# A hand-ordered transformer layer on one core: slots reordered so that rounded products stand together

## The reference

```python
q = (hidden_states @ wq).reshape(b, s, H, D)        # also k, v with 4 heads
q = q * cos + _rotate_half(q) * sin                 # also k
q = q / (jnp.linalg.norm(q, axis=-1, keepdims=True) + EPS) * query_scale
scores = jnp.tanh(scores / CAP) * CAP               # window of 128, softmax
out = jnp.einsum('bhqk,bkhd->bqhd', attn, v).reshape(b, s, H * D)
return out @ wo
```

## Time and profile before

| what | value |
|---|---|
| median of three executions | 858.28 us |
| the profiled execution's own time | 859.33 us |
| its span, first to last instruction | 857.6 us |
| mean granted TensorE clock | 0.985 of full speed |
| TensorE busy (matmul) | 809.3 us, 94%, 5118 instructions |
| VectorE (DVE) | 578.5 us, 67% |
| ScalarE (ACT) | 388.3 us, 45% |
| GpSimd (POOL) | 355.3 us, 41% |
| HBM read and written | 18.47 MB and 2.11 MB, 24 GB/s over the span |

### The profile page before, as it was taken

The page is one execution under the profiler, slowest core; times in us unless marked ns, Lnnn a source line. Parts: engine busy times, 40 slices in busy tenths (PEclk is TensorE's granted clock), DMA queues, the critical chain, the costliest instruction groups (busy, mean ns, idle before and its releaser), DMA issues. The chain is left out here.

```text
span 857.6 us, 14062 instructions
## 1 busy us (share of the span) xinstructions
PE 809.3 (94%) x5118; PEld 716.0 (83%) x5118; DVE 578.5 (67%) x1161; ACT 388.3 (45%) x593; POOL 355.3 (41%) x485
## 2 busy tenths in 40 slices
PE   8889999999999999999999999599979999999996
PEld 7678988988888888888888888498868888888885
DVE  3688688488487577578568576857684565555657
ACT  3565655555555455455455554342322333332321
POOL 2787677477577567568468463100000000000000
PEclk8999999999999999999999999799999999999999
DMA  8200000000000000000000000200300101100001
GB/s 323 88 26 8 27 25 1 2 7 2 1 8 1 1 7 2 1 8 1 1 7 2 2 1 1 74 1 20 104 12 26 37 1 38 37 1 1 2 25 74
DMA packets 7587, 21.48 MB, mean 25 GB/s; under 512 B 1496, under 2 KB 3672, under 8 KB 7392
## 3 DMA queue, kind: packets, MB, share of 16 engines
q1 hardware_dynamic: 6944, 20.31, 7.0%
q10 hardware_dynamic: 576, 0.28, 0.1%
HBM read 18.47 MB, written 2.11 MB: 24 GB/s over the span
## 5 line engine op out<-in xcount | busy, mean ns | idle before, releaser
L574 PE MATMUL ps_o<-vaug,probs 128*128 128x129 f32 x1024 | 136.8, 277 | 16.7 <-DVE o_rows L1050 14.4
L574 PEld LDWEIGHTS ps_o<-vaug,probs 128*128 128x128 f32 x1024 | 128.9, 192 | 26.0 <-issue 18.9
L825 ACT ACTIVATE ps_s<-ps_s 128x1024 f32<-128x1024 f32 x64 | 64.5, 1008 | 127.7 <-PE ps_s L470 127.7
L1046 DVE RECIPROCAL rden<-ps_o 128x2 f32<-128x2 f32 x128 | 21.6, 169 | 146.0 <-PE ps_o L574 145.4
L1350 POOL TENSOR_TENSOR root<-ssq,powers 128x4 f32<-128x4 f32 x80 | 83.3, 1041 | 83.6 <-DVE ssq L1018 83.2
L1361 POOL TENSOR_TENSOR prod<-prod 128x512 f32<-128x512 f32 x80 | 103.0, 1288 | 0.0
L1021 DVE TENSOR_TENSOR prod<-ps_proj,cs 128x1024 f32<-128x1024 f32 x80 | 97.2, 1215 | 0.0
L1366 POOL TENSOR_TENSOR rows<-prod,rnorm 128x512 f32<-128x512 f32 x80 | 89.2, 1115 | 15.5 <-POOL prod L1361 6.0
L468 PE MATMUL ps_proj<-w_hi,h_hi 128*128 128x512 f32 x192 | 83.5, 435 | 1.0 <-DVE w_lo L1001 0.8
L470 PE MATMUL ps_proj<-w_hi,h_lo 128*128 128x512 f32 x192 | 75.9, 395 | 0.0
L468 PE MATMUL ps_y<-wo_hi,oT_hi 128*128 128x256 f32 x256 | 75.7, 296 | 0.1
(11 more groups left out here) (163 smaller groups left out, 2088.3 us busy)
## 6 DMA issues: line engine op xcount, KB each, us to landing
raw_e<-in_we SPq DMA_DIRECT2D x8, 768.0 KB, 4.2
raw_p<-in_wqkv SPq DMA_DIRECT2D x6, 512.0 KB, 7.7
raw_e<-in_wo SPq DMA_DIRECT2D x4, 512.0 KB, 12.4
out<-acc SPq DMA_DIRECT2D x4, 512.0 KB, 2.6
x_all<-in_x SPq DMA_DIRECT2D x1, 1792.0 KB, 7.5
x_all<-in_wmod SPq DMA_DIRECT2D x1, 1024.0 KB, 10.1
gates_a<-gate_rows_dram SPq DMA_DIRECT2D x8, 128.0 KB, 2.9
gates_b<-gate_rows_dram SPq DMA_DIRECT2D x1, 1024.0 KB, 7.9
```

Source lines behind the costliest of these rows:

```text
L574: mm = pe.matmul(ps_o[:, h * (D + 1):(h + 1) * (D + 1)], probs[:, s % 2, at:at + P], vaug[b % 2][:, k, i // 2, :], start=(h == 0 and k == ...
L825: act.activation(ps_s[:], ps_s[:], ACT.Tanh).then_inc(tanh_done, 1)
```

## The change

- `SLOT_TURN`: the turns of rows move to later slots; the last batch has a table of its own, `LAST_TURN`.
- Slots -3 to 2 (`spread`) keep their order, save that `turn_h` moves to the slot's end.
- In all other slots TensorE runs scores, first weighted sum, turn of o, one turn of rows, second weighted sum, all projections and `up`, `down`, output projection, then further turns of rows, `turn_h`, `turn_h2` and the logits. `turn_h2` moves from slot 5 to 6 of a batch, the logits from 6 to 7.
- ACT runs `expo` before `o_head`, and `modulate` and `h_head` at the slot's end.
- DVE normalises both halves before `o_tail`; the sum of squares becomes a function `sums` ahead of `rotate`.
- POOL runs `unit_rows` of all units one slot later, the first ahead of the mask.

The diff, cut to its core:

```diff
--- before.py
+++ after.py
@@ -49,13 +49,15 @@
-SLOT_TURN = [[(0, 5)], [(0, 6)], [(0, 7)], [(0, 8), (0, 9)], [(1, 0)], [(1, 1), (1, 2)], [(1, 3)], [(1, 4)]]
+SLOT_TURN = [[(0, 4)], [(0, 5)], [(0, 6)], [(0, 7)], [(0, 8)], [(0, 9), (1, 0)], [(1, 1), (1, 2)], [(1, 3)]]
...
+LAST_TURN = {ALL - 8: (4, 5), ALL - 7: (6,), ALL - 6: (7,), ALL - 5: (8, 9)}
@@ -107,8 +109,15 @@
+    if s >= ALL - SLOTS:
+        return [(B - 1, r) for r in LAST_TURN.get(s, ())]
...
+def spread(s):
+
+    return s in FIRST_PROJ
@@ -128,10 +137,10 @@
         here = [("o", s - 2)] if live(s - 2) else []
+        here += [("r", b, r) for b, r in turns_of(s)]
         here += [("h", s // SLOTS + 1)] if turns_h(s) else []
-        here += [("r", b, r) for b, r in turns_of(s)]
-        here += [("h2", second(s, 5))] if second(s, 5) is not None else []
-        here += [("l", second(s, 6))] if second(s, 6) is not None else []
+        here += [("h2", second(s, 6))] if second(s, 6) is not None else []
+        here += [("l", second(s, 7))] if second(s, 7) is not None else []
@@ -669,32 +678,47 @@
                 units, turns = units_of(s), turns_of(s)
                 if live(s):
                     scores(s)
-                if live(s - 2):
-                    turn_o(s - 2)
-                if turns_h(s):
-                    turn_h(s // SLOTS + 1)
-                if live(s - 1):
-                    weighted(s - 1, 0)
-                for bb, p in units[:1]:
-                    project(bb, p)
-                for g in SLOT_UP.get(s, ())[:1]:
-                    up(g)
-                if live(s - 1):
-                    weighted(s - 1, 1)
-                for bb, r in turns[:1]:
-                    turn_rows(bb, r)
-                for bb, p in units[1:]:
-                    project(bb, p)
-                for bb, r in turns[1:]:
-                    turn_rows(bb, r)
-                if (b2 := second(s, 5)) is not None:
-                    turn_h2(b2)
-                if (b2 := second(s, 6)) is not None:
-                    router_logits(b2)
+                if spread(s):
+                    if live(s - 2):
+                        turn_o(s - 2)
+                    if live(s - 1):
+                        weighted(s - 1, 0)
+                    for bb, p in units[:1]:
+                        project(bb, p)
+                    if live(s - 1):
+                        weighted(s - 1, 1)
+                    for bb, r in turns[:1]:
+                        turn_rows(bb, r)
+                    for bb, p in units[1:]:
+                        project(bb, p)
+                    for bb, r in turns[1:]:
+                        turn_rows(bb, r)
+                else:
+                    if live(s - 1):
+                        weighted(s - 1, 0)
+                    if live(s - 2):
+                        turn_o(s - 2)
+                    for bb, r in turns[:1]:
+                        turn_rows(bb, r)
+                    if live(s - 1):
+                        weighted(s - 1, 1)
+                    for bb, p in units:
+                        project(bb, p)
+                    for g in SLOT_UP.get(s, ())[:1]:
+                        up(g)
                 for d in SLOT_DOWN.get(s, ()):
                     down(d)
                 if live(s - 2):
                     out_proj(s - 2)
+                for bb, r in turns[1:]:
+                    if not spread(s):
+                        turn_rows(bb, r)
+                if turns_h(s):
+                    turn_h(s // SLOTS + 1)
+                if (b2 := second(s, 6)) is not None:
+                    turn_h2(b2)
+                if (b2 := second(s, 7)) is not None:
+                    router_logits(b2)
                 for g in SLOT_UP.get(s, ())[1:]:
                     up(g)
@@ -897,26 +921,37 @@
...
+                else:
+                    if live(s):
+                        expo(s)
+                    if live(s - 2):
+                        o_head(s - 2)
+                    for bb, r in turns[:1]:
+                        turned(bb, r)
+                    for bb, p in units:
+                        square(bb, p)
+                    for bb, r in turns[1:]:
+                        turned(bb, r)
+                for g in SLOT_UP.get(s, ())[:1]:
+                    gate_of(g)
                 if turns_h(s):
                     modulate(s // SLOTS + 1)
-                if live(s):
...
-                if (b2 := second(s, 5)) is not None:
+                    h_head(s // SLOTS + 1)
+                if (b2 := second(s, 6)) is not None:
                     modulate2(b2)
-                if turns_h(s):
-                    h_head(s // SLOTS + 1)
@@ -1004,6 +1039,15 @@
+            def sums(b, p):
+                if PROJ[p][0] == "v":
+                    return
+                n = NR * b + rot_of(p)
+                dve.wait_ge(square_ready, n + 1)
+                if n >= 2:
+                    dve.wait_ge(root_ready, n - 1)
+                dve.tensor_reduce(ssq[:, n % 2, :], sq[:, n % 2], AX_X, ALU.add).then_inc(summed, 1)
...
@@ -1013,9 +1057,6 @@
-                if n >= 2:
-                    dve.wait_ge(root_ready, n - 1)
-                dve.tensor_reduce(ssq[:, n % 2, :], sq[:, n % 2], AX_X, ALU.add).then_inc(summed, 1)
@@ -1231,31 +1272,51 @@
...
-                if live(s - 1):
-                    normalise(s - 1, 0)
-                if live(s - 2):
-                    o_tail(s - 2)
-                for bb, p in pending:
-                    inverse(bb, p)
-                if live(s - 1):
-                    normalise(s - 1, 1)
-                for bb, p in units[:1]:
-                    rotate(bb, p)
-                for bb, r in turns[:1]:
-                    turned_tail(bb, r)
-                for bb, p in units[:1]:
-                    inverse(bb, p)
-                for bb, p in units[1:]:
-                    rotate(bb, p)
-                for bb, r in turns[1:]:
-                    turned_tail(bb, r)
...
+                else:
+                    for bb, p in pending:
+                        inverse(bb, p)
+                    if live(s - 1):
+                        normalise(s - 1, 0)
+                        normalise(s - 1, 1)
+                    if live(s - 2):
+                        o_tail(s - 2)
+                    for bb, r in turns[:1]:
+                        turned_tail(bb, r)
+                    for n, (bb, p) in enumerate(units):
+                        sums(bb, p)
+                        if n:
+                            inverse(*units[0])
+                        rotate(bb, p)
+                    for bb, r in turns[1:]:
+                        turned_tail(bb, r)
...
-                if (b2 := second(s, 6)) is not None:
+                if (b2 := second(s, 7)) is not None:
                     read_logits(b2)
...
-                return units[1:]
+                return units[1:] if spread(s) else units[-1:]
@@ -1382,16 +1443,17 @@
...
-                for bb, p in pending:
+                for bb, p in pending[:1]:
                     unit_rows(bb, p)
                 if live(s):
                     apply_mask(s)
-                for bb, p in units[:1]:
+                for bb, p in pending[1:]:
+                    unit_rows(bb, p)
+                for n, (bb, p) in enumerate(units):
                     norm_of(bb, p)
-                    unit_rows(bb, p)
-                for bb, p in units[1:]:
-                    norm_of(bb, p)
-                return units[1:]
+                    if spread(s) and n == 0:
+                        unit_rows(bb, p)
+                return units[1:] if spread(s) else units
```

More of the change, by code:

```diff
@@ L899, in slot @@
                     soft(s)
-                if live(s - 2):
-                    o_head(s - 2)
+                if spread(s):
+                    if live(s - 2):
+                        o_head(s - 2)
+                    if live(s):
+                        expo(s)
+                    for bb, p in units[:1]:
+                        square(bb, p)
+                    for bb, r in turns[:1]:
+                        turned(bb, r)
+                    for bb, p in units[1:]:
+                        square(bb, p)
+                    for bb, r in turns[1:]:
+                        turned(bb, r)
+                else:
+                    if live(s):
+                        expo(s)
+                    if live(s - 2):
+                        o_head(s - 2)
+                    for bb, r in turns[:1]:
+                        turned(bb, r)
+                    for bb, p in units:
+                        square(bb, p)
+                    for bb, r in turns[1:]:
+                        turned(bb, r)
+                for g in SLOT_UP.get(s, ())[:1]:
+                    gate_of(g)
                 if turns_h(s):
                     modulate(s // SLOTS + 1)
-                if live(s):
-                    expo(s)
-                for bb, p in units[:1]:
-                    square(bb, p)
```

(13 more changed lines are left out.)

2 lines of the change are left out of this document (removed).

## The result

The changed kernel takes **918.79 us** in the median of four runs (917.42 to 919.04), the kernel before 858.16 beside it: 1.070 times as long, interval 1.068 to 1.071. The prediction had the sign and the main mechanism, but at 891 us (872 to 905) it held little more than half of the loss. The profiled execution took 918.64 us, its span is 916.9, the mean granted clock 0.971 (before 0.985); against the profiled one of before that is +59.3 us of span.

A forecast was written before the change was run, and what follows sets the result against it. TensorE was taken as the bound, busy 63.62 of 65.18 us a batch. Terms 19.6 (six full batches) + 2.5 (batch 0) + 10.5 (last batch) = 32.6 us on 859.33 gave 891.9, 891 on the median; range 872 to 905.

The forecast's parts named there:

- the wait for the single bank: Before w1, the second weighted sum: DVE's answer 1.20 against cover 0.87, so 0.33 us of wait in each slot.
- a wait of 0.17 in one-unit slots: Before the output projection: `o_tail` comes 1.57 after w1's end against one projection of 1.39; none in two-unit slots.
- Rival 1: The waits are mostly covered: 0.33 falls to 0.08 and 0.17 to 0; 873 us, chance 0.13.
- rival 3: Faster: the normalisation fits under the two turns, in slot 2 too, only removals stay; 844 us, chance 0.06.
- a switch of kind: TensorE going from full-precision work to rounded products: 0.00 to 0.02 us each; six fewer a batch, 0.1 us.
- w1 starts at 5.3: Slot 2 of a batch: second weighted sum starts 5.3 us into the slot, wait 2.1 us, slot 9.58.
- slot 5: Slot 5 of a batch: `second_rows` begins near 1.0, second weighted sum at 4.0 (3.5 to 4.3), slot 9.50 us.
- rival 2: The clock falls at the new waits of slots 2, 5 and 60: 8 x 1.65 = 13 us; 904 us, chance 0.11.
- the logits only change slot: Slots 62 to 64, last batch: no turn of rows, 0.76 us each, logits cost nothing more; +2.7 us.
- the ordinary slots: Per batch: slots 0 and 4 7.32 us, 1 and 3 8.54, 5 9.50, 6 8.20, 7 9.44.
- one of the removals: Moving `turn_h` and `turn_h2` to a slot's end ends both waits: 5.7/8 + 5.0/6 = 1.5 us a batch.
- those up to slot 8: Batch 0, old order to slot 2, then losses in slots 3 to 7: +2.5 us.

The follow-up runs named there:

- Experiment 1: Changed kernel with the first projection and up product back between the weighted sums, DVE's `o_tail` back between the normalisations; 867.7 us, ratio 1.011.
- Experiment 3: Kernel before, with the four transposes of single turns of rows spread over the output projection, one ahead of each three products; 870.53 us, ratio 1.014.
- Experiment 5: Changed kernel with twelve dummy products ahead of the second weighted sum in slot 2 of batches 1 to 6; 910.39 us, ratio 1.060.
- Experiment 4: Changed kernel with `modulate2` behind the first expert steps in ACT's queue and `read_logits` behind `accumulate` in DVE's; 911.67 us, ratio 1.062.
- experiment 2: Changed kernel with the old order in every slot; later turns of rows, `turn_h`, `turn_h2` at slot's end and later logits stay; 869.25 us, ratio 1.013.
- experiment 7: Experiment 1 plus `residual` between `o_tail` and second normalisation, the queues of Experiment 4, and last-batch turns one slot later; 849.38 us, ratio 0.989.
- experiment 6: Changed kernel, but in slot 2 of a batch DVE runs `residual` after the first normalisation; 899.04 us, ratio 1.047.

## Why the prediction was wrong in size and right in kind

**Right: the wait for the single bank.** "0.33 us of wait in each slot" is 0.41 in most slots, 0.36 in slot 1 and 0.44 in slot 3; "a wait of 0.17 in one-unit slots" is 0.17 to 0.18. The starts of w1 in slots 60 and 61 came out to within 0.02 us. Experiment 1 shows that this is the cause: with a projection between the sums the waits and 51 us of the loss go. Rival 1, mostly covered, is out, and rival 3 as well: DVE's answer is longer than the two turns that stand over it.

**Right: a switch of kind costs next to nothing.** Experiment 3 gives 0.01 to 0.03 us a run, the text had 0.00 to 0.02. Six fewer a batch are worth 0.2 us at most, against 6 us lost.

**Wrong: "With 0.1 for an `inverse` now ahead of it, w1 starts at 5.3."** The DVE work ahead of the reciprocal was priced by its durations of before, `xn` at the 0.78 that it took beside an idle or lightly loaded POOL. The new order puts it beside POOL's wide product, where it takes 1.68. The prediction had the row that warns of it: the same form of instruction took 2.29 in slot 29, and it used that row for slot 5 only. There the price fell instead, so slot 5 was forecast 0.46 too high, a mistake the other way that hid part of this one. In slot 2 the step costs 1.04 us of wait in each of six batches, 6.2 us.

The Trainium skill, page "SBUF — State Buffer", section "SBUF: two separate sides", says that DVE, in its two-port modes or with two SBUF inputs, and GpSimd share one pair of ports under an exclusive lock, so that the loser blocks for the whole instruction of the other. The trace agrees: the second pass, begun at 265.33 behind POOL's start at 265.21, ends 0.15 us after POOL's product, while that product takes 1.33, near its mean of 1.29. It does not agree for POOL's small `root`: in batch 1 of the kernel before, the second pass began at 119.62, behind `root` at 119.51, and took its 0.40, although `root` ran for 1.06. So not every instruction of POOL blocks for its whole length here, and by the traces the wide product is the neighbour to look for. Whether `xn` runs in a two-port mode no view shows.

**Wrong: the clock as a rival and not as part of the case.** "The 2.1 us are shorter than the 2.67 that the row shows, which speaks against it" hung on the wait that was mis-sized. At 3.14 us it fell in five of six. New half-clock stretches cost, with slot 18's 10.60 as the measure, 2.6 + 1.3 + 1.4 + 1.4 + 1.4 = 8.1 us in slot 2 of the five, 0.81 + 1.97 = 2.8 in slot 60, and 0.72 + 0.97 + 0.81 + 0.79 = 3.3 in slots 63 and 64: 14.2 us, close to the 13 of rival 2. It didn't come in place of the forecast case, but on top of it. Experiment 5 shows the part of slot 2 by itself: 7.9 us, where this reckoning has 8.1. Turns and sums side by side are not enough for a fall: they stand so in the seven other slots of a batch, with 0.36 to 0.44 us of wait, and none of these fell.

**Wrong: "the logits only change slot."** Two waits at the heads of two queues were not looked at. ACT stands 4.07 us for `turn_h2`, DVE 3.44 behind ACT and 5.95 for the logits. In slots 63 and 64 that is 1.58 + 2.72 = 4.3 us of wait more than slot 62 has, with the 3.3 us of clock behind it. Experiment 4 gets 7.1 us back; its two moves were not tried singly.

**Too small: the ordinary slots.** The seven others of a batch are together 0.7 us above the forecast, slot 5's gain counted in: 4.3 us in six. 0.08 of most is the wait for w1. In the slots that begin right behind `turn_h` or the logits the first score product holds the engine 0.32 us in place of 0.23 (247.21 to the next at 247.53).

**Too favourable: one of the removals.** They were put at 1.5 us a batch. The wait of `turn_h`, 0.7 of it, is moved and not saved: it comes back for `h_lo` in slot 3 (experiments 2 and 7), or slot 2 is so long that it hides it. The wait of `turn_h2`, 0.8, is saved with the new order of DVE (experiment 1), though not by the move alone (experiment 2). The slots were summed without either, so this has no line of its own in the sum.

The sum: 32.6 forecast + 14.2 clock + 6.2 slot 2 + 4.3 other slots + 4.3 queues = 61.6, against 59.3. The 2.3 us over lie mostly in three terms forecast 0.7 to 0.8 too high: those up to slot 8 and of slots 58 and 61. Up to slot 8 the eight slots themselves lose 68.4 - 66.1 = 2.3 us, near the 2.5 of the forecast; 0.5 us is gained ahead of slot 0 (its start is 35.98, 36.46 before), and no run says by what. Slots 57 and 58 came out by a path that was only in part foreseen: the turn of rows waits 1.36 us for POOL in slot 57 (0.8 forecast, 1.2 its upper bound) and 2.85 in slot 58, where the forecast had w1 waiting for DVE. That the three slots 56 to 58 together cost 3.0 us where 3.2 were forecast is luck. The +2.7 of slots 62 to 64 is 0.4 more than three times its own 0.76. The range ended at 905 because each mechanism was priced alone; the case in which the wait is a microsecond longer and the clock falls on it was not in it.

## What to carry to other kernels

A product that two uses of one bank stand around is a cover: before moving it, compare the partner engine's answer (here 1.28 us) with what is left over it (0.87). When an order moves, price the partner engine's instructions by the row in which the same neighbour runs, not by their own of before, and let a wait of a length that may bring a fall of the clock (here 2.24 us already did) be priced with the fall. For each turn or product that goes to a later slot, look for its reader, and for what stands behind that reader in its queue.

## What was not expected of the hardware

- The same wait of 3.14 us brought the clock to 0.50 in five batches and not in the sixth; in experiment 4, where slot 2 is the same, it fell in all six. Three batches of six fell at 2.24 us (experiment 1); none fell at 0.86 or at 1.0 (experiments 6 and 2). What tells the batches apart stays open. Once the fall lasted 6.8 us in place of 3.4.
- One pass of `xn` took 402 ns and the next, of the same form, 1361 ns beside POOL's wide product. In experiment 7 the update of `x_all`, with two inputs, took 1.66 us beside two of POOL's wide instructions, and 0.69 in the kernel before.
- A wait shown as 0.24 us was one of 0.41, since the modelled ends of the matmuls before it reach into it. Starts told it, the list of waits did not.
